# Spreading the count sums of the build over the units of a pair of chunks: 14 blocks of 2 or 4 matmuls instead of 5 blocks of 10

## The reference, cut to what matters

```
# x: (3125, 128), src, dst: (103125,), edge_weight: (103125,)
agg = segment_sum(x[src], dst)                                  # layer 0, round 0 of the kernel
h   = max((x + agg) @ W1 + b1, 0) @ W2 + b2 + x @ Wres + bres
x   = layernorm(x + h)
# layer 1: two mean aggregations over the same edges             (rounds 1, 2)
# layer 2: four steps with edge-weighted, normalised sums        (rounds 3 to 6)
#          neigh = zeros.at[dst].add(norm[:, None] * h[src])
# layer 3: one more sum over the same edges, with edge features  (round 7)
```

## Time and profile before

| | |
|---|---|
| median of 3 runs | 1219.0 us (1217.5 to 1220.62) |
| the profiled execution | 1217.5 us, of which 1215.7 us are the span from the first to the last instruction |
| PE busy | 1070.6 us (88%) |
| DVE busy | 555.6 us (46%) |
| ACT busy | 285.4 us (23%) |
| the build on PE (L1263 and L1239) | from 119.5 us to 337 us |
| PE busy with L1263 in all / L1239 in all | 106.5 us in 6500 matmuls / 85.8 us in 650 |

### The profile page before, as it was taken

The page is one execution under the profiler, slowest core; times in us unless marked ns, Lnnn a source line. Parts: engine busy times, 40 slices in busy tenths (PEclk is TensorE's granted clock), DMA queues, the critical chain, the costliest instruction groups (busy, mean ns, idle before and its releaser), DMA issues.

```text
span 1215.7 us, 25749 instructions
## 1 busy us (share of the span) xinstructions
PE 1070.6 (88%) x10720; PEld 638.1 (52%) x10720; DVE 555.6 (46%) x1066; ACT 285.4 (23%) x579; POOL 102.9 (8%) x92
## 2 busy tenths in 40 slices
PE   5013688888889999999999999999999999999898
PEld 4013577777765454444445644546454555446454
DVE  1866789999764333551222322233223233543323
ACT  2013689888831101101000000000000001212100
POOL 4884000000000000000000000000000000000000
PEclk9555699999999999999999999999999999999999
DMA  5421466777797567566775897749986499653951
GB/s 152 146 61 43 167 250 290 296 303 296 303 387 306 206 263 276 196 258 273 294 281 198 334 382 290 310 164 365 367 316 264 182 375 388 250 225 140 427 199 30
DMA packets 39238, 311.56 MB, mean 256 GB/s; under 512 B 10873, under 2 KB 13161, under 8 KB 17298
## 3 DMA queue, kind: packets, MB, share of 16 engines
q1 hardware_dynamic: 27983, 298.70, 62.6%
q0 software_dynamic: 11200, 12.09, 3.6%
HBM read 245.45 MB, written 65.24 MB: 256 GB/s over the span
## 4 chain that ended last, share of the span: by engine, by line
PE 72%; DMA 11%; POOL 5%; DVE 4%; issue 4%; ACT 1%; SPq 0%; DVEq 0%; ACTq 0%; POOLq 0%
PE ps L1153 43%; PE ps L1143 15%; DMA weight_mats<-arena 11%; PE ps L1100 4%; POOL arena L436 3%; POOL arena L444 3%; PE ps L1239 2%; PE ps L1056 2%; PE ps L1263 2%; PE ps L1113 1%; PE ps L1052 1%; PE ps L1005 1%; DVE arena L711 1%; DVE arena L712 1%; DVE arena L709 1%
## 5 line engine op out<-in xcount | busy, mean ns | idle before, releaser
L1153 PE MATMUL ps<-arena 125*128 125x500 f32 (+1 forms) x700 | 269.4, 540 | 0.0
L1153 PE MATMUL ps<-arena,parts_even 125*128 125x500 f32 (+1 forms) x700 | 267.7, 538 | 0.0
L1153 PEld LDWEIGHTS ps<-arena 125*128 125x128 f32 x700 | 123.5, 190 | 128.4 <-issue 128.4
L1153 PEld LDWEIGHTS ps<-arena,parts_even 125*128 125x128 f32 x700 | 122.9, 189 | 127.4 <-issue 127.4
L1143 PE MATMUL ps<-arena 125*128 125x500 f16 (+2 forms) x700 | 141.1, 353 | 4.8 <-issue 4.2
L1263 PE MATMUL ps<-arena 64*128 64x52 f16 (+1 forms) x6500 | 106.5, 181 | 34.6 <-DVE arena L643 21.3
L927 ACT ACTIVATE arena<-ps 128x400 f16<-128x400 f32 (+1 forms) x195 | 125.3, 642 | 37.6 <-PE ps L1263 23.1
L1263 PEld LDWEIGHTS ps<-arena 64*128 64x128 f16 x6500 | 96.4, 95 | 52.2 <-ACT arena L929 28.5
L913 ACT ACTIVATE XT<-ps 128x500 f32<-128x500 f32 (+1 forms) x49 | 26.5, 541 | 399.5 <-PE ps L1113 399.4
L929 ACT ACTIVATE arena<-ps 128x400 f32<-128x400 f32 (+1 forms) x195 | 118.0, 605 | 0.0
L638 DVE TENSOR_TENSOR arena<-arena 128x4224 f16<-128x4224 f16 (+2 forms) x52 | 116.3, 2236 | 0.0
(11 more groups left out here) (177 smaller groups left out, 837.4 us busy)
## 6 DMA issues: line engine op xcount, KB each, us to landing
arena<-weight_mats SPq DMA_DIRECT2D x24, 3250.0 KB, 11.5
arena<-weight_mats SPq DMA_DIRECT2D x24, 3000.0 KB, 10.9
arena<-count_mats SPq DMA_DIRECT2D x18, 3125.0 KB, 11.0
weight_mats<-arena SPq DMA_DIRECT2D x13, 3125.0 KB, 14.4
count_mats<-arena SPq DMA_DIRECT2D x13, 1562.5 KB, 6.0
arena<-weight_mats SPq DMA_DIRECT2D x4, 1625.0 KB, 6.4
arena<-weight_mats SPq DMA_DIRECT2D x4, 1500.0 KB, 6.2
arena<-count_mats SPq DMA_DIRECT2D x3, 1562.5 KB, 6.4
```

The source lines that it names most:

```text
L1153: ins = t.matmul(o, xs[:, k, :], rhs, start=(k == 0), stop=(k == NC - 1))
```

## The change

The 25 steps of `sum_counts` are no longer put before every third unit in fives. Each of the units 1 to 14 gets its share before its own matmuls: `a, z = (u-1)*25//14, u*25//14`, which is one step (2 matmuls) before the units 1, 5 and 10 and two steps (4 matmuls) before the eleven others. Number, form and order of the steps among each other are the same, and so are all waits. The last block stands before unit 14 instead of unit 13. The sums of the last pair, behind the loop, are not touched.

```diff
@@ -1249,8 +1249,9 @@
                         if counts is not None:
                             if u == 1:
                                 pe.wait_ge(counts_out, UNITS * q)
-                            if u % SLOTS3 == 1:
-                                sum_counts(q - 1, counts, range(KCH * (u // SLOTS3), KCH * (u // SLOTS3) + KCH))
+                            if u:
+                                a, z = ((u - 1 + d) * NC // (UNITS - 1) for d in (0, 1))
+                                sum_counts(q - 1, counts, range(a, z))
                         if UNIT_AT[u] == STEP_AT[step]:
                             pe.wait_ge(hots_ok, STEPS * q + step + 1)
                         pe.wait_ge(weights_out, UNITS * q + u - SLOTS3 + 1 + OUT_PAD)
```

## The result

The changed kernel takes 1227.33 us (median of 5 runs, 1222.25 to 1231.22), the kernel before 1219.0. The ratio is 1.0063, 95% interval 1.0034 to 1.0094. The forecast was 1220.0 with a range of 1217 to 1224, and 0.80 for "same": the change costs 8 us where 1 was expected.

The account below looks back on a forecast made before the run. The prediction took weight stores in series, 15.85 us a round, to bound the build. Middle 0, last pair 0.25, pair 2 0.45 and first pass 0.3 gave +1.0 us on 1219.0, so 1220.0, range 1217 to 1224.

Parts of the forecast that it names:

- What bounds the kernel before: Middle of the build: weight stores one after the other, a round of 15.85 us; no engine computes on the path.
- cover: The store's round of 15.85 us, under which PE's 14.4, ACT's 14.1 and DVE's 15.1 us were to stay hidden.
- The price of a block: On PE, each block of count matmuls costs 0.18 to 0.19 us beside its matmuls, for changing form and back.
- second rival: Short blocks cost much more than those of ten and PE replaces the store as bound: about 1235 us, chance 0.11.
- Middle, 9 rounds: 0: Nine middle rounds of the build: no change, since all engines stay under the store's round of 15.85 us.
- third rival: PE gets the low clock after idling in every pair and overruns the store's round: about 1224 us, chance 0.05.
- Last pair: End of the build: unit 14 is done later and ACT waits for it, so the end slips 0.25 us.
- Pair 2: Loop's second pass: PE ends unit 14 after ACT could start on it, so the store is 0.45 us later.
- First pass: Loop's first pass (pair 1), where PE stalls for code: +0.3 us, between 0 and +1.6.
- fourth rival: First pass loses its stalls, 6.1 us in all, as code is used evenly: about 1216 us, chance 0.05.

Follow-up runs that it names:

- e3: Kernel before, but SP issues each pair's store without waiting for the landing of the one before (overlapped stores): 1217.06 us, ratio 0.9991.
- e1: Kernel before with its five blocks of five steps moved early, ahead of units 1, 3, 5, 8 and 10: 1241.59 us, ratio 1.0194.
- e4: Changed kernel with overlapped stores, each issued without waiting for the landing of the one before: 1230.22 us, ratio 1.0088 against the kernel before.
- e5: Changed kernel plus seven filler matmuls, result unread, at the end of each pass of PE's loop: 1223.36 us, ratio 1.0039 against the kernel before.
- e9: Changed kernel's fourteen blocks with overlapped stores and seven filler matmuls per pass: 1222.62 us, ratio 1.0024 against the kernel before.
- e2: Kernel before with fourteen blocks, mostly late: one step ahead of units 1 to 11, then 5, 5, 4 ahead of 12 to 14: 1229.61 us, ratio 1.01.
- e7: As e2, but ACT takes the sum out before its copies of unit 14, not behind them: 1221.12 us, ratio 1.0029 against the kernel before.
- e10: Kernel before with overlapped stores and four blocks: 4, 6, 5, 10 steps ahead of units 1, 4, 8, 12, no filler: 1231.94 us, ratio 1.0106.
- e6: Kernel before with overlapped stores and nine filler matmuls at the end of each pass of PE's loop: 1211.7 us, ratio 0.9938.

## Why the prediction was wrong

- **What bounds the kernel before: right.** The stores in series did (e3: 15.0 us a round without them), and the change could show only past their cover.
- **The price of a block: right.** 0.18 to 0.19 us was forecast. Measured: 0.53 us for a block of four with its change of form, 0.10 over 4 x 0.108, and 0.56 for a unit of 36 with the change back, 0.09 over 36 x 0.013. So the second rival (short blocks cost much more) is refuted. It is the same with blocks of two matmuls (0.32 us from 228.20 to 228.52, 0.10 over 2 x 0.108) as with ten. The Trainium skill's "TensorEngine Tiling (Array Packing)", section Key Properties, says that a change of the tiling mode drains the engine; that each change costs time agrees with it, but no run shows how much of it is the drain.
- **"Middle, 9 rounds: 0": the step that failed.** I set each engine's whole work per pair (PE 14.4, DVE 15.1 us) against the store's 15.85 and found room (DVE's is 14.8: the 145 instructions of the earlier trace rows are 9.1 pairs, not 8.9; that changes nothing here). But PE and DVE don't work beside each other all the time: DVE's step 0 of the next pair waits for PE's unit 11, and PE's unit 0 for that step. The ring is PE from unit 0 to unit 11 plus 4.4 us (4.3 by the chain above), and the rows for it were there. Before: 400 x 0.013 + 20 x 0.216 + 4 x 0.18 + 4.4 = 14.6. After: 19 steps and 11 blocks, 5.2 + 4.1 + 2.0 + 4.4 = 15.7, measured 15.91. Seven of the nine new blocks lie in this ring. That is level with the stores, with nothing left to cover anything. e1, e4, e5 and e9 show it.
- **The clock, my third rival with 0.05: right in kind, wrong in weight and size.** I had let a slow round overrun by 0.4 us, because I thought that 1.4 us of cover were left; with none left it costs all of its 1.2. In the profiled execution four of ten rounds had it, 4.8 of the 5.6 us of the middle; e5 takes them away. My argument against it, that PE would have less idle time, counted the sum of the idle time and not the one gap ahead of unit 0, which stayed (1.15 us after, 1.31 before).
- **Last pair, +0.25 forecast: 2.6 measured.** The addition from unit 3 on was right (it is 13.2 us from there to the last sums; before 12.9), but I let it start where the freed buffer let it start before. With PE's lead over the stores used up by the ring, unit 3 starts 4.0 us after the buffer could have been free (the store issued at 309.89 us, 14.5 us on), and not 1.2.
- **Pair 2, +0.45 forecast: +0.8 measured. First pass, +0.3: +0.1.** Both within their bounds. ACT did get unit 1 earlier (no wait of 2.34 us there) and gained nothing by it.
- **The fourth rival** (fewer stalls in the first pass) didn't happen: the pass took 24.9 us against 24.8, with stalls of 1.35, 3.88 and 1.90 us, 7.1 in all against 6.1.

The spread of the runs fits the same two causes: each slow round now adds 1.2 us, and in how many it falls can differ from run to run. The clock granted over a whole run goes with its time in e4 (1223.68 us at 0.946, 1233.01 at 0.935) and in the changed kernel (1222.25 at 0.946, 1231.22 at 0.940). It isn't all of the spread: e9, whose profiled build has no slow round, spans 7.8 us in 12 runs. What decides in which rounds the low clock falls with gaps of 1.15 us stays open. With 2.24 us (e1) it was every round, with 1.3 to 1.5 us (e3) three of eleven, with 0.8 (e2) and 0.3 us (e5) none.

## What to carry to other kernels

A cover is to be compared with the longest ring of waits that passes through the changed engine, not with the engines' busy times: follow each semaphore back until it closes, and add up only what lies between. Work placed ahead of the ring's last release is paid in every round. The same work behind it costs nothing in that ring, but it can lengthen another one, as in e2, e7 and e10, so all rings have to be added up. And where a new bound is level with the old one, whatever the old one hid (here, a low clock after idle time) comes back at its full price.

## What the runs showed of the hardware that I had not expected

- A gap of 1.15 us on PE ahead of each round was enough to bring the low clock in four of ten rounds, and the round was 1.2 us longer; with seven useless matmuls in it, which left 0.3 us of the gap, no round had it. Adding work to PE made the changed kernel 4 us faster (e5), or 7.6 us with overlapped stores (e9 against e4), and the kernel before 5 us with overlapped stores (e6 against e3).
- A change between matmuls on 64-row tiles and on all rows costs 0.09 to 0.10 us each way at the high clock, whether two, four or ten matmuls lie between.
